# The first expert mixture as single-expert tiles, rows sent by indirect transfers

## The reference

```python
def _L0_ffn_ref(x, w_router, W1, b1, W2, b2, Ws1, bs1, Ws2, bs2):
    logits = jnp.einsum('btd,ed->bte', x, w_router)          # 8 experts
    probs = jax.nn.softmax(logits, axis=-1)
    vals, idx = jax.lax.top_k(probs, 2)
    gates = jnp.sum(jax.nn.one_hot(idx, 8) * vals[..., None], axis=-2)
    hs = gelu(jnp.einsum('btd,fd->btf', x, Ws1) + bs1)       # d_ff 512
    acc = jnp.einsum('btf,df->btd', hs, Ws2) + bs2
    h = gelu(jnp.einsum('btd,efd->btef', x, W1) + b1)
    y = jnp.einsum('btef,edf->bted', h, W2) + b2
    return SCALE * (acc + jnp.einsum('bted,bte->btd', y, gates))
```

## Time and profile before

| | |
|---|---|
| runs | 1186.05, 1193.46, 1195.53 us (median 1193.46) |
| profiled execution: its time | 1186.87 us |
| profiled execution: its span | 1185.6 us |
| TensorE (PE) busy | 976.0 us, 82% |
| VectorE (DVE) busy | 782.7 us, 66% |
| ScalarE (ACT) busy | 589.5 us, 50% |
| GpSimd (POOL) busy | 245.0 us, 21% |
| moved by DMA | 62.49 MB, mean 53 GB/s |

### The profile page before, as it was taken

How to read it: one execution, slowest core, us unless ns; L and a number is a source line. 1 busy time by engine, 2 the same in 40 slices (tenths; PEclk the granted TensorE clock), 3 DMA queues, 4 the chain that set the end, 5 groups by cost and what they waited for, 6 DMA issues and landing times.

```text
span 1185.6 us, 20975 instructions
## 1 busy us (share of the span) xinstructions
PE 976.0 (82%) x8169; PEld 552.0 (47%) x8169; DVE 782.7 (66%) x1990; ACT 589.5 (50%) x1019; POOL 245.0 (21%) x321
## 2 busy tenths in 40 slices
PE   6777779998999975767658999999578688689999
PEld 4233334444676752545433334566223233357667
DVE  7786888821326479878678963867787877664512
ACT  2556546674335347778627785223045456343342
POOL 2843220000000235967420000001120001100000
PEclk9898979998999985878877999999568889989999
DMA  8324250000000310491125007101003000100000
GB/s 315 103 71 94 63 188 2 3 5 1 1 1 1 107 37 1 143 182 54 47 68 185 2 3 107 43 1 44 11 28 134 2 1 2 36 1 1 10 1 10
DMA packets 35894, 62.49 MB, mean 53 GB/s; under 512 B 5235, under 2 KB 25668, under 8 KB 34196
## 3 DMA queue, kind: packets, MB, share of 16 engines
q1 hardware_dynamic: 33828, 58.64, 17.5%
q10 hardware_dynamic: 1968, 2.51, 0.8%
HBM read 43.04 MB, written 16.65 MB: 50 GB/s over the span
## 4 chain that ended last, share of the span: by engine, by line
PE 57%; DVE 28%; ACT 5%; POOL 4%; issue 3%; DMA 2%; SPq 1%; ACTq 0%; POOLq 0%; DVEq 0%
PE ps_s L970 10%; PE ps_e L960 10%; PE ps_v L759 7%; DVE mx L1999 6%; PE ps_e L649 4%; PE ps_e L1065 2%; DVE mx L1991 2%; PE ps_s L1052 2%; DVE ps_s L1973 2%; ACT work L1495 2%; PE ps_e L664 2%; DVE xn L1943 2%; PE ps_s L679 2%; DVE stats L1925 1%; DVE work L2532 1%
## 5 line engine op out<-in xcount | busy, mean ns | idle before, releaser
L1495 ACT ACTIVATE work<-ps_e 128x512 f32<-128x512 f32 x406 | 223.1, 597 | 110.5 <-PE ps_e L649 105.5
L2772 POOL TENSOR_TENSOR rstd<-rstd,halves 128x2 f32<-128x2 f32 x52 | 36.7, 706 | 657.4 <-DVE rstd L1930 657.0
L1999 DVE TENSOR_REDUCE mx<-ps_s 128x2 f32<-128x1024 f32 x128 | 153.6, 1221 | 21.0 <-PE ps_s L679 18.8
L1602 ACT ACTIVATE work<-ps_s,keep 128x512 f32<-128x512 f32 x136 | 93.0, 687 | 139.2 <-PE ps_s L970 136.1
L759 PE MATMUL ps_v<-work,vaug 128*32 128x256 f32 x1536 | 128.0, 408 | 5.0 <-ACT work L1483 4.9
L649 PE MATMUL ps_e<-q_stack,ctx_stack 52*128 52x256 bf16 (+1 forms) x684 | 121.7, 291 | 9.2 <-DMA q_stack<-mT 3.3
L960 PEld LDWEIGHTS ps_e<-ffn_w,work 128*128 128x128 f32 x960 | 117.2, 195 | 21.3 <-issue 19.6
L679 PE MATMUL ps_s<-ctx_stack,q_stack 49*128 49x512 bf16 (+1 forms) x296 | 91.6, 450 | 40.7 <-DVE mx L1999 30.7
L2198 DVE SCALAR_TENSOR_TENSOR x<-ps_e,gates,x 128x128 f32<-128x128 f32 x128 | 38.9, 346 | 124.8 <-PE ps_e L960 119.1
L970 PE MATMUL ps_s<-xnT,ffn_w 128*128 128x512 f32 x240 | 117.6, 614 | 3.6 <-ACT work L1602 3.6
L960 PE MATMUL ps_e<-ffn_w,work 128*128 128x128 f32 x960 | 119.3, 279 | 0.8 <-DVE x L2188 0.8
(11 more groups left out here) (412 smaller groups left out, 1965.9 us busy)
## 6 DMA issues: line engine op xcount, KB each, us to landing
q_stack<-q_scr SPq DMA_DIRECT2D x32, 192.0 KB
ffn_w<-in_L0f_w SPq DMA_DIRECT2D x1, 4608.0 KB, 17.5
ffn_w<-in_L1f_w SPq DMA_DIRECT2D x1, 3456.0 KB, 13.0
q_scr<-parts SPq DMA_DIRECT2D x16, 192.0 KB, 2.1
c_scr<-ffn_w SPq DMA_DIRECT2D x12, 256.0 KB, 7.6
kx_scr<-ffn_w SPq DMA_DIRECT2D x12, 256.0 KB, 3.9
ctx_stack<-kx_scr SPq DMA_DIRECT2D x2, 1536.0 KB
ctx_stack<-c_scr SPq DMA_DIRECT2D x2, 1536.0 KB
```

The costliest lines, as they stand in the source:

```text
L1495: act.activation(pt[:, parity, :, :].rearrange("p k q -> p (k q)"), bank[exp_bank(use, h, parity)], ACT.Exp).then_inc(exped, 1)
L1602: act.activation(hid_unit(st, u)[:, j, :], bank[f"h{n % 2}"], ACT.Gelu_apprx_tanh, bias=b1).then_inc(HIDS[st], 1)
L1999: m = dve.tensor_reduce(mx[:, b, :, pair, part], ps_s[i][:], AX, ALU.max, negate=True)
```

## The change

Half g of the rows (batches 2g and 2g + 1) now goes only to the two experts that each row chose. `rank` (TensorE) and `destinations` (VectorE) work out for each row and choice a place in a buffer of 15 tiles of 128 rows (`TILES`), each tile belonging to one expert, and which expert that is (`expert_i`). POOL sends the normed rows there by eight indirect DMAs of 128 rows each (`scatter`, to `x_sent` in DRAM, which SP has filled with zeros), SP reads the 15 tiles back in one DMA of 960 KB (`fetch_sent`), TensorE turns them (`turn_sent`), and `tile_up` and `tile_down` run the one expert of each tile, eight products of 128x128 in all. SP loads the expert numbers into registers (`owners`) and fetches each tile's weights (514 KB) from DRAM into a ring of four (`fetch_tile`). ScalarE applies gelu in four instructions a tile and copies each four tiles of results out of PSUM (`evacuate`); SP stores them (`store_block`) and POOL gathers each row's two results by eight indirect DMAs (`gather`), which `combine` on VectorE adds into x with the gates. The shared expert stays dense: `shared_up` four times and `shared_down` twice a half. Of `l1_early`, q 0 to 9 stand behind the tiles 5 to 14 of the second half and q 10 to 35 behind all tiles on TensorE and ScalarE; on VectorE all stand between `combine(1)` and `combine(2)`. The order of POOL and SP is in the diff. Some semaphores of earlier stages are used again under new names (`after(signal, n)` is the signal's count raised by n).

The diff, cut to its core:

```diff
+TILES = 2 * B * S // 2 // P + NE - 1
+RING = 4
+TILE_W = 2 * FH + FJ
+BLOCKS0 = -(-TILES // 4)
+SHARED_BEFORE = {88: 1, 89: 1, 90: 1, 91: 1}
+RANK0 = 71
+RANK1 = 3
+GATES0 = 7
+EARLY_A1 = 5
...
+        def rank(g):
+            claim("m")
+            pe.wait_ge(*after(ranked, g + 1))
+            pe.matmul(ps_m[:, 0:32], before_b, chosen_b[:, 0:32], start=True, stop=False, skip_group_check=True)
+            for t in range(3):
+                pe.matmul(ps_m[:, (t + 1) * NE:4 * NE], all_b, chosen_b[:, 0:(3 - t) * NE], start=False, stop=t == 2,
+                          skip_group_check=True)
+            for t in range(4):
+                m = pe.matmul(ps_m[:, 4 * NE:5 * NE], all_b, chosen_b[:, t * NE:(t + 1) * NE], start=t == 0, stop=t == 3,
+                              skip_group_check=True)
+            m.then_inc(rank_ps[0], 1)
+            free["m"] = after(destined, g + 1)
...
+        def turn_sent(g, q):
+            name = ("v", "m")[q % 2]
+            claim(name)
+            if q == 0:
+                pe.wait_ge(*after(x_there, 16 * (g + 1)))
+            for i in range(4 * q, min(4 * q + 4, TILES)):
+                m = pe.transpose(bank[name][:, i % 4 * P:(i % 4 + 1) * P], xg[:, i, :], ident)
+            m.then_inc(turned_x_ps[0], 1)
+            free[name] = after(turned_x, BLOCKS0 * g + q + 1)
...
+        def tile_up(g, i):
+            n, at = UP_USE["tile", g, i], g * TILES + i
+            name, w = f"h{n % 2}", tile_ring[at % RING]
+            claim(name)
+            pe.wait_ge(*after(tile_there[at % RING], 16 * (at // RING + 1)))
+            if i % 4 == 0:
+                pe.wait_ge(*after(turned_x, BLOCKS0 * g + i // 4 + 1))
+            for j in range(FJ):
+                m = pe.matmul(bank[name][:, j * P:(j + 1) * P], w[:, j * P:(j + 1) * P], xgT[:, i, :],
+                              start=True, stop=True)
+            m.then_inc(up_ps, 1)
+            free[name] = (hidden, n + 1)
+
+        def tile_down(g, i):
+            at = g * TILES + i
+            name, w, hid = f"e{i // 4 % 2}", tile_ring[at % RING], tile_hid[at % RING]
+            if i % 4 == 0:
+                claim(name)
+            pe.wait_ge(hidden, UP_USE["tile", g, i] + 1)
+            for j in range(FJ):
+                m = pe.matmul(bank[name][:, i % 4 * P:(i % 4 + 1) * P], hid[:, j, :], w[:, FH + j * E:FH + (j + 1) * E],
+                              start=(j == 0), stop=(j == FJ - 1))
+            m.then_inc(tile_ps[0], 1)
+            free[name] = after(evacuated, BLOCKS0 * g + i // 4 + 1)
...
+            shared_down(0)
+            shared_down(1)
+            for q in range(BLOCKS0):
+                turn_sent(0, q)
+            for g in range(2):
+                tile_up(g, 0)
+                tile_up(g, 1)
+                for i in range(TILES):
+                    if i + 2 < TILES:
+                        tile_up(g, i + 2)
+                    tile_down(g, i)
+                    if g == 0 and i == RANK1:
+                        rank(1)
+                    if g == 0 and i == GATES0:
+                        turn_gates("L0f", NE + 1, 1, ROUTE_AT["L0f"] + 1, "v")
+                        gated_bias("L0f", 0, NE + 1, 1, "m")
+                    if g == 1 and i >= EARLY_A1:
+                        l1_early(i - EARLY_A1)
+                if g == 0:
+                    for j in range(FJ):
+                        shared_up(1, j)
+                    for q in range(BLOCKS0):
+                        turn_sent(1, q)
+                    shared_down(2)
+                    shared_down(3)
+            for q in range(TILES - EARLY_A1, 36):
+                l1_early(q)
...
+        def tile_gelu(g, i):
+            n, at = UP_USE["tile", g, i], g * TILES + i
+            w, hid = tile_ring[at % RING], tile_hid[at % RING]
+            if at >= RING:
+                act.wait_ge(*after(tile_ps, at - RING + 1))
+            act.wait_ge(up_ps, n + 1)
+            for j in range(FJ):
+                m = act.activation(hid[:, j, :], bank[f"h{n % 2}"][:, j * P:(j + 1) * P], ACT.Gelu_apprx_tanh,
+                                   bias=w[:, 2 * FH + j:2 * FH + j + 1])
+            m.then_inc(hidden, 1)
+
+        def evacuate(g, k):
+            last = min(4 * k + 4, TILES)
+            n = (last - 4 * k) * P
+            if g == 1 and k == 0:
+                act.wait_ge(*after(y_stored, 16 * BLOCKS0))
+            act.wait_ge(*after(tile_ps, g * TILES + last))
+            act.activation(y_tile[:, k, 0:n], bank[f"e{k % 2}"][:, 0:n], ACT.Copy).then_inc(evacuated[0], 1)
...
+        def destinations(g, ts):
+            flat = parts[:].rearrange("p s t -> p (s t)").bitcast(F32)[:, TOK:TOK + 8 * NT * NE]
+            o1, o2 = route_tmp(2)[:, ts], route_tmp(3)[:, ts]
+            passed = flat[:, 0:TILES * NE].rearrange("p (i e) -> p i e", e=NE)
+            pairs = flat[:, 256:320].rearrange("p (e f) -> p e f", e=NE)
+            place = flat[:, 320:352].rearrange("p (t e) -> p t e", e=NE)
+            both = flat[:, 384:448].rearrange("p (c t e) -> p c t e", c=2, e=NE)
+            n_tiles, end, base, dest, owner = (flat[:, 448 + 8 * i:456 + 8 * i] for i in range(5))
+            owner = flat[:, 480:480 + TILES]
+            within, count = ps_m[:, 0:4 * NE].rearrange("p (t e) -> p t e", e=NE), ps_m[:, 4 * NE:5 * NE]
+            dve.wait_ge(*after(rank_ps, g + 1))
+            settle(dve.tensor_scalar(n_tiles, count, 0.5, None, ALU.is_gt))
+            for i in range(1, 4):
+                settle(dve.scalar_tensor_tensor(n_tiles, count, i * P + 0.5, n_tiles, ALU.is_gt, ALU.add))
+            settle(dve.tensor_tensor(pairs, n_tiles.unsqueeze(1).broadcast_to([P, NE, NE]), upto, ALU.mult))
+            settle(dve.tensor_reduce(end, pairs, AX, ALU.add))
+            settle(dve.tensor_tensor(base, end, n_tiles, ALU.subtract))
+            settle(dve.tensor_scalar(base, base, float(P), None, ALU.mult))
+            settle(dve.tensor_tensor(place, within, base.unsqueeze(1).broadcast_to([P, 4, NE]), ALU.add))
+            dve.tensor_tensor(both[:, 0], o1, place, ALU.mult)
+            settle(dve.tensor_tensor(both[:, 1], o2, place, ALU.mult))
+            settle(dve.tensor_reduce(dest, both.rearrange("p c t e -> p (c t) e"), AX, ALU.add))
+            settle(dve.tensor_copy(dest_i[:, g, :], dest))
+            settle(dve.tensor_tensor(passed, numbers.unsqueeze(2).broadcast_to([P, TILES, NE]),
+                                     end.unsqueeze(1).broadcast_to([P, TILES, NE]), ALU.is_ge))
+            settle(dve.tensor_reduce(owner, passed, AX, ALU.add))
+            dve.tensor_scalar(expert_i[:, g, 0:TILES], owner, NE - 1.0, None, ALU.min).then_inc(destined[0], 1)
...
+        def combine(b):
+            g = b // 2
+            dve.wait_ge(*after(y_gathered, 128 * (g + 1)))
+            dve.wait_ge(down_x, b + 1)
+            for c in range(2):
+                for t in tiles(b):
+                    m = dve.scalar_tensor_tensor(x[:, t, :], y_rows[:, g, c, t % 4, :], top_gates[:, c, t:t + 1],
+                                                 x[:, t, :], ALU.mult, ALU.add)
+                if c == 0:
+                    settle(m)
+            m.then_inc(combined[0], 1)
...
+            shared_add(0)
+            shared_add(1)
+            for q in range(BLOCKS0):
+                turned_sent(0, q)
+            route_rest("L0f", None, 1, slice(4, 8))
+            destinations(1, slice(4, 8))
+            turn_gates("L0f", NE + 1, 1, "v")
+            gated_bias("L0f", 1, "m")
+            for q in range(BLOCKS0):
+                turned_sent(1, q)
+            shared_add(2)
+            shared_add(3)
+            for b in (0, 1):
+                combine(b)
+                statistics(A1, b)
+                normalised(A1, b)
+            for q in range(36):
+                l1_early(q)
...
+        def scatter(g):
+            pool.wait_ge(*after(destined, g + 1))
+            pool.wait_ge(*after(zeroed, 32))
+            if g == 1:
+                pool.wait_ge(*after(x_scattered, 128))
+            for t in range(4):
+                for c in range(2):
+                    pool.indirect_dma_start(
+                        out=x_sent[g][:, :],
+                        out_offset=bass.IndirectOffsetOnAxis(ap=dest_i[:, g, c * 4 + t:c * 4 + t + 1], axis=0),
+                        in_=xn[:, 4 * g + t, :], in_offset=None).then_inc(x_scattered[0], 16)
+
+        def gather(g):
+            pool.wait_ge(*after(y_stored, 16 * BLOCKS0 * (g + 1)))
+            if g == 1:
+                pool.wait_ge(*after(y_gathered, 128))
+            for t in range(4):
+                for c in range(2):
+                    pool.indirect_dma_start(
+                        out=y_rows[:, g, c, t, :], out_offset=None, in_=y_sent[g][:, :],
+                        in_offset=bass.IndirectOffsetOnAxis(ap=dest_i[:, g, c * 4 + t:c * 4 + t + 1], axis=0),
+                    ).then_inc(y_gathered[0], 16)
...
+            gather(1)
...
```

(54 more changed lines are left out.)

259 lines of the change are left out of this document (156 added, 103 removed).

## The result

The changed kernel took 1222.33 us (median of 4 runs, 1219.24 to 1228.93), the kernel before, on the same chip, 1190.95 (median of 4). The ratio is 1.0272, 95% interval 1.0208 to 1.0335: slower, by 31 us where I had forecast 12.5. The profiled execution has a span of 1219.7 us.

What follows compares the result with a forecast made beforehand. TensorE (82% busy) was taken to bound the kernel; start, loops, pause and formerly hidden steps put the hand-over at 447.5 against 434.6, +12.9 rounded to +12.5, giving 1206.0 us on the 1193.46 median; range 1180 to 1238.

Steps and rivals of the forecast that it cites:

- my own case: The forecast itself, +12.5 us to 1206.0, with its own range 1191 to 1226; chance 0.60.
- second rival: The low clock holds through both tile loops, a tile taking 3.56 us: +17 over the sum, 1226; chance 0.12.
- The hand-over: VectorE's norm of batch 3, ending the mixture: 434.6 before, forecast 447.5; its shift taken as the change of the time.
- The start: Up to the first tile at 298.0: -4 for ups removed, +3.2 for rank and destinations holding bank `m`.
- Loop 1: First half's 15 tiles, waiting for weight fetches: 39.0 us, 298.0 to 337.0, against 26.7 with free fetches.
- L: Time from a ring place's release to its new contents in the tile loops: 3.8 us, bounds 3.0 to 5.1.
- the clock's share: Effect of the granted clock on the sum; its part of the own range was -7 to +6.
- Between the halves: Row fetch issued 2.2 us after the last down (1.6 to 5), 10.5 us until 347.5; turns and shared downs to 354.1.
- Loop 2: Second half's tiles: again 39 us, plus 3 for three activation table changes of 1.28, ending at 396.1.
- Behind the loop: Early steps, near scores, roots and combines formerly hidden, from the last tile to batch 3's norm: 44.4 us.
- the first (fetches covered, TensorE's pace): Both loops run at TensorE's pace, falling by 12.3 each, and the clock stays up: -16, 1177.5; chance 0.15.
- The third: POOL needs long for the indirect DMAs, from 2.5 us each; at 4 each +33 over the sum, 1238; chance 0.13.

Runs made afterwards that it cites:

- again: The changed kernel run once more, unchanged, in group 2: 1221.2 us, ratio 1.0128 to 1.0309 to the kernel before.
- all3: Changed kernel with six ring places, second half's rows fetched early with expert numbers loaded singly, and sixteen early steps in the loop: 1182.59 us, ratio 0.9899.
- sent_early: Changed kernel with each second-half expert number loaded just before its fetch and that half's rows fetched after the first half's last fetch: 1226.0 us.
- direct: Changed kernel with all 32 indirect transfers made plain ones of the same bytes from GpSimd's queue: 1225.1 us.
- early2: Changed kernel with early steps from tile 1 of the second half, two a tile, twenty in the loop, first two batches' transfers inside it: 1221.1 us.
- ring6: Changed kernel with six weight ring places in place of four: 1212.8 us, ratio 1.0133 to 1.0226 to the kernel before.
- late_early: Kernel before with early steps 10 to 35 moved behind the dense mixture: 1222.15 us, ratio 1.026.

## Why the prediction was right in kind and short in size

The forecast was slower (chance 0.54) by 12.5 us, and 31 were measured: the direction and the places of the losses were right, the sum was less than half. The 1222 lies in the range of my own case (1191 to 1226), near its upper end. It also lies closer to the second rival's 1226 than to my 1206, and by another mechanism than that one. The hand-over was forecast at 447.5 and came at 463.7. The 16.2 us between divide so:

- **The start**, 298.0 forecast, 302.5 measured: +4.5. 2.6 us were there before the scatter. They are chance: between 80 and 100 us this execution was granted 0.52, the kernel before 0.87 and `again` 1.00, with the same code. The rank stall was about 2.5 (GpSimd's roots are 2.6 late ahead of it, 5.1 behind; forecast 3.2). TensorE waits 2.30 for bank `m` in `again` and `all3` too, but there the granted clock falls to 0.51 behind the wait (252 to 256 in `again`) and the stall costs 5.1 in all, more than my bound of 4. The two shared downs ran at a clock of 0.61 (293 to 301) and took 6.3 in place of 3.6.
- **Loop 1**, 41.2 with its share of the clock, 44.5 measured: +3.3. L was right (3.7 to 3.9 alone), and at a granted clock of 1.00 two tiles took 5.7 to 5.9 us where the formula without the clock gives 5.6. The clock that I had added was mostly not lost: 1.00 was granted up to 332 us, and 0.81 from there to 339.5, which cost one pair 1.6. So the clock's share of my sum stood by luck for something else, the second half's gate products, which I had left out. They stood in the loop: TensorE waits 0.9 in their middle and the tiles lose 2.5. The first `down` ends 0.8 later than I had it.
- **Between the halves**, 19.8 with turns, downs and clock, 23.2 measured: +3.4. "2.2 us until it is issued (1.6 to 5)" is the step that was mis-sized: 5.5, outside its own bounds, because of the register loads. I had named their price (9 us, the issue 3 us later) and left it out of the sum; it was 8.7 and 3.3. From the issue to TensorE's first turn passed 10.0 in place of 8.3, and turns and downs took 7.7 in place of 9.3. `sent_early` and `all3` show that the 14 us are SyncE's order and not the scatter's time.
- **Loop 2**, 44.1, 47.2 measured: +3.1. The table loads came as forecast (three of 1.28, the last `down` idle for 3.69); the fetches that overlapped took longer than L, and again the clock was 1.00 (371 to 408), so that its share stood in for them.
- **Behind the loop**, 44.4, 46.3 measured: +1.9. 14.0 to the near scores (forecast 13.8), then 2.06 a step in place of 1.68, at a granted clock of 0.50.

Then 5 us behind the hand-over point, where I had let its shift stand for the whole. That was sound: `all3`, `direct` and `early2` keep their shift from there to the end within 1 us. The 5, like the 2.6 ahead of the scatter, are this execution's clock. One term, the issue of the row fetch, lies outside its bounds; the others are each short by 2 to 5 us and all in the same direction, which makes up the rest.

The rivals: the first (fetches covered, TensorE's pace) is what `ring6` and `all3` are, and not the changed kernel. The second is excluded: 0.91 to 1.00 was granted in the windows that lie wholly in the loops. The third fell in its form, GpSimd took 0.96 us for one indirect DMA and 1.27 from one to the next, 10.2 for the first eight, where I had 10.4. In its result it is half right, for a reason that it doesn't name: in two of three groups waits end late beside scatters and gathers, which is worth 33 us and more where the transfers are doubled and about half of that where they aren't. That GpSimd waits for a VectorE copy (the rule of the Trainium skill, SBUF — State Buffer, that I had weighed) isn't seen: the pitch stays 1.25 to 1.27 in all four groups of eight, but VectorE worked little beside them, so this tests the rule weakly.

What the change gained isn't lost in one place: the loops are 92 us with their waits where 53 would do, the pause is 23, and steps that the dense mixture had covered lie bare, which alone costs the kernel before 31 us (`late_early`).

## What to carry to other kernels

A ring's slack is counted in work, not in places: four places gave one tile, 1.8 us, against the 3.7 from release to new contents, and two more places brought each tile to TensorE's pace. When a stage is made shorter, ask what ran in its shadow, and price it bare: here it cost as much as the whole saving. And look at an in-order DMA engine as at any other: register loads and stores that stand ahead of a transfer are part of its latency. Last, before a difference of a few us between two executions is put down to a change, look at the stretches whose code is the same: here they differ by up to 12 us.
